# Batch attention of a four-layer tower: who forms the elementwise products, and where the weighted sums stand on TensorE

## The chip, the cores and the metric

The program runs on one core of a Trainium2 chip, in one launch. Its engines are TensorE (PE: matmuls, with weight loads as PEld), VectorE (DVE), ScalarE (ACT), GpSimd (POOL) and SyncE (SP). They run side by side and wait for each other by semaphores. The metric is device time in microseconds. The kernel before was timed three times: 2326.43, 2315.5 and 2321.1 us, median 2321.1 us.

## The reference, cut to what matters

The model is a tower of eight layers on activations `h` of 8 sequences x 512 tokens x 128. The change touches the seventh alone, an attention of 8 heads of 16. Its first axis is called the sequence, but it receives the 8 sequences as that axis, so each of the 512 token positions attends among 8 vectors only:

```python
def _L3_attn_ref(emb, W, b):
    L, B, E = emb.shape                      # 8, 512, 128
    scaling = (E / N_HEAD) ** (-0.5)
    ft = jnp.einsum('lbe,oe->lbo', emb, W) + b
    ft = ft.reshape(L, B * N_HEAD, 3 * HEAD_DIM).transpose(1, 0, 2)
    q, k, v = jnp.split(ft, 3, axis=-1)
    scores = jnp.einsum('bld,bmd->blm', q, k) * scaling
    mask = scores == 0
    attn = jax.nn.softmax(jnp.where(mask, -jnp.inf, scores), axis=-1)
    attn = jnp.where(mask, jnp.zeros((), attn.dtype), attn)
    out = jnp.einsum('blm,bmd->bld', attn, v)
    return out.transpose(1, 0, 2).reshape(L, B, E)
...
h = h + _L3_attn_ref(_layernorm(h, axis=-1), L3_attn_W, L3_attn_b)
```

## The kernel before, in words

`batch_attention` works in four chunks `c` of 128 token positions. An 8 x 8 attention per position and head is too small for a matmul, so it is done with elementwise products and sums:

- **Key products** (L2174): for each query `l` of 8, one DVE multiplication of the keys of all 8 positions `m` with query `l`, 128 x 1024 numbers, into `KM`. The first four of chunk 0 are made at the end of the layer before.
- **Scores** (L2293): TensorE sums each product over the 16 numbers of a head, by a matmul with a window of ones (`head_win`). One group of eight matmuls for `l` 0 to 3 (half 0), one for `l` 4 to 7 (half 1), both into the bank `SP`.
- ScalarE copies the scores out (L2240), TensorE turns them by four transposes (L2303), and VectorE runs the softmax (L2193 to L2203), with the exponential on ScalarE (L2244).
- **Weighted values** (L2209): for each `l`, one DVE multiplication of the values with the weights, 128 x 1024, into `big`.
- **Sums** (L2313): eight matmuls with the identity for each half, one for each `m` (called `k` in the code), add the products over `m` in a bank of PSUM. VectorE adds the bank to `h` (L2162).
- For chunk c+1 the layer norm is computed on VectorE beside this (L147 to L161, then `vector_scale`, L168), with a power on GpSimd (L184). TensorE then turns the normed tiles and projects to queries, keys and values (L2262 to L2279), and ScalarE copies them out (L2221 to L2235).

Nothing here is scheduled by a planner: each engine's queue is the order in which the code is written, and an instruction that waits holds up all behind it. On VectorE chunk c's queue is: key products of c, statistics of c+1, the two additions of c-1, `vector_scale` of c+1, softmax of c, weighted values of c. On TensorE it is: scores of c, transposes, projection of c+1, all 16 sums of c. GpSimd has nothing but the power. In the text, T0 is the moment at which a chunk's first weighted value starts on VectorE, right after L2203.

Of the kernel before, what the change touches and what calls it, by code (L numbers as in the profile page):

```python
# [16 lines left out]
ALU = mybir.AluOpType  # L17
# [3 lines left out]
P = 128  # L21
B, T, D = 8, 512, 128
NC_ = T // P
NT = B * NC_
NH = 8
DH = D // NH
# [2073 lines left out]
def batch_attention(ctx, nc, m):  # L2100
# [22 lines left out]
    norm = Norm(ctx, nc, m, "ba")  # L2123
    xt_ps, xt_sb, q_ps, q_sb, k_ps, k_sb, v_ps, v_sb = (sig(n, 2) for n in ("xt_ps", "xt_sb", "q_ps", "q_sb", "k_ps", "k_sb", "v_ps", "v_sb"))
    qk, sc_ps, sh_sb, sct_ps, st, ex_in, ex_sb = sig("qk", L), sig("sc_ps", 2), sig("sh_sb", 1), sig("sct_ps", 1), sig("st", 8), sig("ex_in", 1), sig("ex_sb", 1)
    pv, sum_ps, h_sb = sig("pv", L), sig("sum_ps", 2), sig("h_sb", 2)
    norm_m = Norm(ctx, nc, m, "cp")
    MX = [m.big[:, s * T:(s + 1) * T].rearrange("p (c d) -> p c d", c=NC_) for s in S]
# [4 lines left out]
    lmh = lambda v: v.rearrange("p (l m h) -> p l m h", l=L, m=L)  # L2133

    XC = [m.t512c[1][:, s, :] for s in S]
    made = lambda c, k: qk.at(c, k) - L // 2

    def chunk(c):

# [3 lines left out]
    with nc.Block() as block:  # L2143
# [4 lines left out]

        @block.gpsimd
        def _(pool):  # L2150
            for c in range(1, NC_):
                norm.gpsimd(pool, c - 1)
            norm_m.gpsimd(pool, 0)

        @block.vector
        def _(dve):

            def add(c):
                for half in S:
                    dve.wait_ge(sum_ps.sem, sum_ps.at(c, half + 1))  # L2160
                    h = H4[:, 4 * half:4 * half + 4, c, :]
                    nc.vector.tensor_tensor(h, h, OUT[half][:, :].rearrange("p (l d) -> p l d", d=D), ALU.add).then_inc(h_sb.sem, 1)  # L2162
                    if c == NC_ - 1 and half == 0:
                        dve.wait_ge(h_sb.sem, h_sb.at(c, 1))
                        norm_m.vector(dve, 0, norm_m.pair(0), MX)

            for c in range(NC_):
                for l in range(0 if c else L // 2, L):
                    if c and l % 4 == 0:
                        dve.wait_ge(q_sb.sem, q_sb.at(c - 1, l // 4 + 1))  # L2170
                    if c and l == 0:
                        dve.wait_ge(k_sb.sem, k_sb.at(c - 1, 2))
                        dve.wait_ge(sc_ps.sem, sc_ps.at(c - 1, 2))
                    nc.vector.tensor_tensor(QK[l].rearrange("p (m t) -> p m t", m=L), KT.rearrange("p (m t) -> p m t", m=L),  # L2174
                                            QT[:, l * P:(l + 1) * P].rearrange("p (o t) -> p o t", o=1).broadcast_to([P, L, P]),
                                            ALU.mult).then_inc(qk.sem, 1)
                if c + 1 < NC_:
                    norm.vector_stats(dve, c, chunk(c + 1))
                    norm.vector_aggr(dve, c)
                if c:  # L2180
                    add(c - 1)
                if c + 1 < NC_:
                    norm.vector_scale(dve, c, chunk(c + 1), XN)

                n = [0]

                def link(ins):
                    n[0] += 1
                    ins.then_inc(st.sem, 1)
                    dve.wait_ge(st.sem, st.at(c, n[0]))  # L2190

                dve.wait_ge(sct_ps.sem, sct_ps.at(c, 1))
                link(nc.vector.tensor_scalar(MK, SPT[:, :], 0.0, None, ALU.is_equal))  # L2193
                link(nc.vector.scalar_tensor_tensor(SC, MK, -3e38, SPT[:, :], ALU.mult, ALU.add))
                link(nc.vector.tensor_reduce(by_lh(mx[:, :]), by_m(SC), AX.X, ALU.max))
                nc.vector.tensor_tensor(lmh(SC), lmh(SC), wide_m(mx[:, :]), ALU.subtract).then_inc(ex_in.sem, 1)
                link(nc.vector.tensor_scalar(some[:, :], mx[:, :], -1e38, None, ALU.is_gt))
                dve.wait_ge(ex_in.sem, ex_in.at(c, 1))
                dve.wait_ge(ex_sb.sem, ex_sb.at(c, 1))
                link(nc.vector.tensor_reduce(by_lh(mx[:, :]), by_m(EX), AX.X, ALU.add))  # L2200
                link(nc.vector.reciprocal(mx[:, :], mx[:, :]))
                link(nc.vector.tensor_tensor(mx[:, :], mx[:, :], some[:, :], ALU.mult))
                link(nc.vector.tensor_tensor(lmh(EX), lmh(EX), wide_m(mx[:, :]), ALU.mult))  # L2203
                dve.wait_ge(v_sb.sem, v_sb.at(c, 2))
                for l in range(L):
                    pl = EX[:, slot(l) * L * NH:(slot(l) + 1) * L * NH].rearrange("p (n o) -> p n o", o=1).broadcast_to([P, L * NH, DH])
                    if c and l % 4 == 0:
                        dve.wait_ge(sum_ps.sem, sum_ps.at(c - 1, l // 4 + 1))
                    nc.vector.tensor_tensor(PR[l].rearrange("p (n x) -> p n x", x=DH), V[c % 2].rearrange("p (n x) -> p n x", x=DH),  # L2209
                                            pl, ALU.mult).then_inc(pv.sem, 1)  # L2210
            add(NC_ - 1)
            dve.wait_ge(h_sb.sem, h_sb.at(NC_ - 1, 2))

        @block.scalar
        def _(act):
# [22 lines left out]
            for c in range(NC_):  # L2238
                act.wait_ge(sc_ps.sem, sc_ps.at(c, 2))
                nc.scalar.copy(SH, SP[:, :]).then_inc(sh_sb.sem, 1)  # L2240
                if c + 1 < NC_:
                    turned(c + 1)
                act.wait_ge(ex_in.sem, ex_in.at(c, 1))
                nc.scalar.activation(EX, SC, ACT.Exp, scale=DH ** -0.5).then_inc(ex_sb.sem, 1)  # L2244
                if c + 1 < NC_:
                    project(c + 1)
            for s in S:
                act.wait_ge(mt_ps.sem, s + 1)
# [3 lines left out]
        def _(pe):  # L2252
# [3 lines left out]
            def project(c):  # L2256
# [12 lines left out]
                    nc.tensor.matmul(KP[s][:, :], w["b_w"][:, D:2 * D], XT[s][:, :], start=True, stop=True).then_inc(k_ps.sem, 1)  # L2269
                values(c)  # L2270

            def values(c):
                for s in S:
                    if c:
# [8 lines left out]

            for c in range(NC_):
                for half in S:
                    if c or half:
                        pe.wait_ge(qk.sem, made(c, 4 * half + 4))
                    if c and half == 0:
                        pe.wait_ge(sh_sb.sem, sh_sb.at(c - 1, 1))
                    for b in S:  # L2290
                        o = 24 - 16 * half - 8 * b
                        for g in range(4):
                            last = nc.tensor.matmul(SP[32 * g:32 * g + 32, :], w["head_win"][:, o:o + 32],  # L2293
                                                    QK[4 * half + g].rearrange("p (a b t) -> p a b t", b=2, t=P)[:, :, b, :],
                                                    start=half == 0 and b == 0, stop=half == 1 and b == 1)
                    last.then_inc(sc_ps.sem, 1)
                    if c == 0 and half == 0:
                        values(0)
                pe.wait_ge(sh_sb.sem, sh_sb.at(c, 1))
# [4 lines left out]
                last.then_inc(sct_ps.sem, 1)  # L2304
                if c + 1 < NC_:
                    project(c + 1)
                for half in S:
                    pe.wait_ge(pv.sem, pv.at(c, 4 * half + 4))
                    if c:
                        pe.wait_ge(h_sb.sem, h_sb.at(c - 1, half + 1))  # L2310
                    every = m.big[:, 4 * half * L * D:4 * (half + 1) * L * D].rearrange("p (l m d) -> p l m d", l=4, m=L)
                    for k in range(L):
                        last = nc.tensor.matmul(OUT[half][:, :].rearrange("p (l d) -> p l d", d=D), w["ident"][:, :], every[:, :, k, :],  # L2313
                                                start=k == 0, stop=k == L - 1)
                    last.then_inc(sum_ps.sem, 1)
            for s in S:
                pe.wait_ge(norm_m.ready.sem, s + 1)
                for k in range(NC_):
# [559 lines left out]
```

## Time and profile before

| | |
|---|---|
| median of 3 runs | 2321.1 us |
| the profiled execution, its span | 2301.55 us, 2300.5 us |
| busy PE, DVE, ACT, POOL | 81%, 76%, 57%, 14% |
| instructions | 31597 |
| mean granted TensorE clock | 0.9 of full |
| the batch attention, from the first key product to the last transposes | 1869.0 to 2007.7 us |

The batch attention is 6% of the span. The profile's page is an average over eight layers and says little of it, so the rows below are of its stretch, and of the few places elsewhere where GpSimd runs elementwise instructions beside VectorE. Each line of a timeline begins with the start and the length in us; one line may hold several instructions (x8), and its end in brackets is the idle time of the engine just before it and what released it. Where a matmul is of 32-bit floats each appears as two instructions, so 16 sums are x32.

### The profile page before, as it was taken

How to read it: one execution, taken by the hardware profiler on the slowest of the kernel's cores; microseconds unless marked ns; L12 is line 12 of the kernel's file. 1: busy time of each engine (PE TensorE's matmuls, PEld its weight loads, DVE VectorE, ACT ScalarE, POOL GpSimd, SP SyncE). 2: the span in 40 equal slices, each digit the busy share in tenths (PEclk: the TensorE clock that was granted, in tenths of full speed). 3: DMA queues.
4: the chain of work that ended last, by engine and by line, in shares of the span. 5: the costliest groups of instructions: out<-in, count | busy, mean ns of one | idle time of the engine just before them, and what ended most of it. 6: DMA issues, size and time to landing. Idle time of an engine off the chain costs nothing. (4 is left out here: it accounts for less than half of the span.)

```text
span 2300.5 us, 31597 instructions
## 1 busy us (share of the span) xinstructions
PE 1857.3 (81%) x11676; PEld 960.1 (42%) x11676; DVE 1748.0 (76%) x4911; ACT 1316.6 (57%) x1459; POOL 327.9 (14%) x392
## 2 busy tenths in 40 slices
PE   4999998888766688999989999899999979654930
PEld 1566654676421123344333344333344554332620
DVE  1677557577777789999999999999999778784532
ACT  0222222222236999999999999999999721010310
POOL 6000012010234000000000000000000000055256
PEclk8889999787688999999999999999999989867975
DMA  5400000000001100000000000000000000042632
GB/s 181 161 1 18 21 1 29 1 1 1 1 0 33 65 1 1 1 1 1 1 1 1 1 1 1 1 1 1 1 1 1 1 4 1 5 178 79 198 96 73
DMA packets 39658, 67.08 MB, mean 29 GB/s; under 512 B 7744, under 2 KB 27728, under 8 KB 38736
## 3 DMA queue, kind: packets, MB, share of 16 engines
q1 hardware_dynamic: 30768, 41.96, 5.4%
q0 software_dynamic: 8736, 23.10, 3.2%
q8 instruction: 93, 1.52, 0.3%
q14 instruction: 61, 0.50, 0.1%
HBM read 39.87 MB, written 23.07 MB: 27 GB/s over the span
## 5 line engine op out<-in xcount | busy, mean ns | idle before, releaser
L1929 ACT ACTIVATE KM<-KM 128x2048 f32<-128x2048 f32 x290 | 538.8, 1908 | 8.0 <-DMA w_a_ba<-in_a_ba 7.2
L1754 DVE TENSOR_SCALAR KM<-big 128x512 f32<-128x512 f32 x1160 | 480.3, 482 | 35.4 <-PE bank L2067 29.1
L2067 PE MATMUL bank<-KM,w_a_wa 128*32 128x512 f32 x2736 | 377.8, 626 | 90.7 <-ACT KM L1929 69.2
L184 POOL TENSOR_TENSOR nrstd<-nrstd,minus_half 128x4 f32<-128x4 f32 (+1 forms) x80 | 82.3, 1050 | 1759.9 <-DVE nrstd L161 1759.7
L1929 ACT ACTIVATE aa_args<-aa_args 128x2048 f32<-128x2048 f32 x142 | 266.0, 1909 | 1.5 <-DVE aa_args L1754 1.5
L1754 DVE TENSOR_SCALAR aa_args<-big 128x512 f32<-128x512 f32 x568 | 236.1, 482 | 12.9 <-PE bank L2067 12.3
L2067 PE MATMUL bank<-aa_args,w_a_wa 128*32 128x512 f32 x1360 | 185.7, 619 | 43.6 <-ACT aa_args L1929 31.3
L2067 PEld LDWEIGHTS bank<-KM,w_a_wa 128*32 128x32 f32 x2736 | 54.7, 109 | 240.9 <-ACT KM L1929 136.9
L2039 PE MATMUL bank<-XT,rf_wgu 128*128 128x256 f32 x512 | 145.0, 406 | 0.0
L2033 PE MATMUL bank<-XT,rf_wgu 128*128 128x256 f32 x512 | 142.7, 401 | 2.3 <-DVE ST L1825 2.3
L1926 ACT ACTIVATE KM<-big 128x512 f32<-128x512 f32 x208 | 132.8, 717 | 0.0
L2039 PEld LDWEIGHTS bank<-XT,rf_wgu 128*128 128x128 f32 x512 | 88.8, 193 | 97.8 <-issue 78.1
L2033 PEld LDWEIGHTS bank<-XT,rf_wgu 128*128 128x128 f32 x512 | 87.7, 189 | 94.9 <-issue 84.7
L1825 DVE SCALAR_TENSOR_TENSOR ST<-ST,bank 128x512 f32<-128x512 f32 x128 | 87.6, 684 | 46.2 <-ACT ST L1919 45.9
L1919 ACT ACTIVATE ST<-bank 128x512 f32<-128x512 f32 x128 | 75.8, 592 | 48.8 <-PE bank L2039 48.8
L2027 PEld LDWEIGHTS bank<-rf_wd,ST 128*128 128x128 f32 x512 | 62.3, 191 | 49.8 <-issue 48.3
L2313 PE MATMUL bank<-big,w_ident 128*128 128x512 f32 x128 | 63.3, 657 | 20.8 <-DVE big L2209 20.8
L2027 PEld LDWEIGHTS bank<-rf_wd,t512b 128*128 128x128 f32 x512 | 63.3, 193 | 37.3 <-issue 36.9
L1838 DVE SCALAR_TENSOR_TENSOR h<-bank,rf_w,h 128x128 f32<-128x128 f32 x256 | 77.4, 345 | 0.7 <-PE bank L2027 0.7
L583 ACT COPY KM<-bank 128x512 f32<-128x512 f32 x32 | 17.2, 593 | 104.2 <-PE bank L743 104.2
L2067 PEld LDWEIGHTS bank<-aa_args,w_a_wa 128*32 128x32 f32 x1360 | 27.0, 108 | 117.9 <-ACT aa_args L1929 69.6
L2027 PE MATMUL bank<-rf_wd,ST 128*128 128x128 f32 x512 | 73.6, 287 | 0.8 <-DVE ST L1831 0.8
(405 smaller groups left out, 3116.2 us busy)
## 6 DMA issues: line engine op xcount, KB each, us to landing
queues<-zeros SPq DMA_DIRECT2D x1, 8192.0 KB, 25.3
KM<-queues SPq DMA_DIRECT2D x32, 256.0 KB, 3.0
results<-KM POOLq DMA_DIRECT2D x32, 256.0 KB, 3.4
w<-in_w SPq DMA_DIRECT2D x1, 4096.0 KB
big<-in_w_pairs SPq DMA_DIRECT2D x1, 4096.0 KB
mf_tv<-in_task_W SPq DMA_DIRECT2D x1, 2048.0 KB, 8.4
la_v<-in_task_W SPq DMA_DIRECT2D x1, 2048.0 KB, 8.7
big<-XN SPq DMA_DIRECT2D x8, 256.0 KB, 2.6
```

The costliest lines, as they stand in the source:

```text
L184: self.nc.gpsimd.tensor_tensor(self.m.nrstd[s][:, 0:self.tiles], self.m.nrstd[s][:, 0:self.tiles], self.m.minus_half[:, 0:self.tiles], ALU ...
L1754: last = nc.vector.tensor_scalar(ARG(n, step)[:, cc, :], KU[:, i * T:(i + 1) * T], q, None, ALU.add)
L1825: nc.vector.scalar_tensor_tensor(TH(e), TH(e), 1.0, GATE(e)[:, :], ALU.add, ALU.mult).then_inc(a1_sb.sem, 1)
L1838: last = nc.vector.scalar_tensor_tensor(h, OUT(e)[:, s * D:(s + 1) * D], WT[:, s, e:e + 1], h, ALU.mult, ALU.add)
L1919: nc.scalar.activation(TH(e), GATE(e)[:, :], ACT.Tanh, scale=0.5).then_inc(th_sb.sem, 1)
L1926: last = nc.scalar.activation(ARG(n, step)[:, cc, :], KU[:, i * T:(i + 1) * T], ACT.Tanh, bias=query(n, step, cc))
L1929: last = nc.scalar.activation(ARG(n, step), ARG(n, step), ACT.Tanh)
L2027: last = nc.tensor.matmul(OUT(e)[:, s * D:(s + 1) * D], AC(e)[:, o:o + P], wd[:, e, a, :], start=a == 0, stop=a == HB - 1)
L2033: last = nc.tensor.matmul(LIFT(e)[:, a * TOK:(a + 1) * TOK], wgu[:, e, 1, a, :], XMT[parity][:, 0:TOK], start=True, stop=True)
L2039: last = nc.tensor.matmul(GATE(e)[:, a * TOK:(a + 1) * TOK], wgu[:, e, 0, a, :], XMT[parity][:, 0:TOK], start=True, stop=True)
L2067: last = nc.tensor.matmul(m.bank[g][32 * cc:32 * cc + 32, :], w["a_wa"][:, 30 - 2 * k:62 - 2 * k], ARG(n, step)[:, cc, :], start=k == 0, s ...
L2313: last = nc.tensor.matmul(OUT[half][:, :].rearrange("p (l d) -> p l d", d=D), w["ident"][:, :], every[:, :, k, :], start=k == 0, stop=k == ...
```

## The change

Two of the eight key products (`l` = 3 and 7, list `PL`) and two of the eight weighted values of each chunk go from VectorE to GpSimd. The first group of chunk 0 stays on VectorE. GpSimd's products signal by semaphores of their own (`qk_pool`, `pv_pool`), for which TensorE and ScalarE now wait too. The 16 sums of a chunk, which stood in one piece, are divided: all of half 0 and the first two of half 1 stay in their place, three go behind the first group of the next chunk's scores and three behind the second. After the last chunk all 16 still stand together.

```diff
+    qk_pool, pv_pool = sig("qk_pool", 2), sig("pv_pool", 2)
+    DL, PL = [l for l in range(L) if l % 4 != 3], [3, 7]
-    made = lambda c, k: qk.at(c, k) - L // 2
+    made = lambda c, half: L // 2 + len(DL) * (c - 1) + len(DL) // 2 * (half + 1)
         def _(pool):
-            for c in range(1, NC_):
-                norm.gpsimd(pool, c - 1)
+            for c in range(NC_):
+                if c:
+                    for half, l in enumerate(PL):
+                        pool.wait_ge(q_sb.sem, q_sb.at(c - 1, half + 1))
+                        if half == 0:
+                            pool.wait_ge(k_sb.sem, k_sb.at(c - 1, 2))
+                            pool.wait_ge(sc_ps.sem, sc_ps.at(c - 1, 2))
+                        nc.gpsimd.tensor_tensor(QK[l]..., KT..., QT..., ALU.mult).then_inc(qk_pool.sem, 1)
+                if c + 1 < NC_:
+                    norm.gpsimd(pool, c)
+                for half, l in enumerate(PL):
+                    if half == 0:
+                        pool.wait_ge(st.sem, st.at(c, 8))
+                        pool.wait_ge(v_sb.sem, v_sb.at(c, 2))
+                    if c:
+                        pool.wait_ge(sum_ps.sem, sum_ps.at(c - 1, half + 1))
+                    nc.gpsimd.tensor_tensor(PR[l]..., V[c % 2]..., pl, ALU.mult).then_inc(pv_pool.sem, 1)
...
-                for l in range(0 if c else L // 2, L):
+                for l in (DL if c else range(L // 2, L)):
...
-                for l in range(L):
+                for l in DL:
...
+                if c:
+                    act.wait_ge(pv_pool.sem, pv_pool.at(c - 1, 2))
                 nc.scalar.activation(EX, SC, ACT.Exp, scale=DH ** -0.5).then_inc(ex_sb.sem, 1)
                 if c + 1 < NC_:
+                    if c:
+                        act.wait_ge(qk_pool.sem, qk_pool.at(c - 1, 2))
                     project(c + 1)
...
+            def sums(c, half, ks):
+                every = m.big[:, 4 * half * L * D:4 * (half + 1) * L * D]...
+                for k in ks:
+                    if k == 0:
+                        pe.wait_ge(pv.sem, len(DL) * c + len(DL) // 2 * (half + 1))
+                        pe.wait_ge(pv_pool.sem, pv_pool.at(c, half + 1))
+                        if c:
+                            pe.wait_ge(h_sb.sem, h_sb.at(c - 1, half + 1))
+                    last = nc.tensor.matmul(OUT[half]..., w["ident"][:, :], every[:, :, k, :], start=k == 0, stop=k == L - 1)
+                if k == L - 1:
+                    last.then_inc(sum_ps.sem, 1)
...
                 for half in S:
-                    if c or half:
-                        pe.wait_ge(qk.sem, made(c, 4 * half + 4))
+                    if c:
+                        pe.wait_ge(qk.sem, made(c, half))
+                        pe.wait_ge(qk_pool.sem, qk_pool.at(c - 1, half + 1))
...
                     last.then_inc(sc_ps.sem, 1)
+                    if c:
+                        sums(c - 1, 1, ((2, 3, 4), (5, 6, 7))[half])
...
-                for half in S:
-                    pe.wait_ge(pv.sem, pv.at(c, 4 * half + 4))
...
+                sums(c, 0, range(L))
+                sums(c, 1, (0, 1) if c + 1 < NC_ else range(L))
```

On TensorE, from the end of a projection to the next, the queue before reads as follows (L2279 is the projection's last matmul, L2313 the sums, L2293 the scores, L2303 the transposes of the scores, L2262 those of the next projection):

```order
L2279 MATMUL bank<-w_b_b,w_first_row 128x512
L2313 MATMUL bank<-big,w_ident 128x512 x16
L2293 MATMUL bank<-KM,w_head_win 32x512 x16
L2303 MATMUL bank<-w_ident,t512b 128x8x16 x4
L2262 MATMUL bank<-w_ident,XN 128x128 x8
```

The same place in the changed program's queue on TensorE (the sums are now L2305 and the scores L2334):

```order
L2317 MATMUL bank<-w_b_b,w_first_row 128x512
L2305 MATMUL bank<-big,w_ident 128x512 x10
L2334 MATMUL bank<-KM,w_head_win 32x512 x8
L2305 MATMUL bank<-big,w_ident 128x512 x3
L2334 MATMUL bank<-KM,w_head_win 32x512 x8
L2305 MATMUL bank<-big,w_ident 128x512 x3
L2346 MATMUL bank<-w_ident,t512b 128x8x16 x4
L2287 MATMUL bank<-w_ident,XN 128x128 x8
```

Six of the sixteen sums now stand behind scores, and the last three of them ahead of the transposes.

On GpSimd, in the whole of the layer, only powers stood (first row below); in the changed program the products stand between them (L2172 weighted values, L2160 key products):

```order
-L184 TENSOR_TENSOR nrstd<-nrstd,minus_half 128x4 x8
+L184 TENSOR_TENSOR nrstd<-nrstd,minus_half 128x4 x2
+L2172 TENSOR_TENSOR big<-big,t512b 128x1024 x2
+L2160 TENSOR_TENSOR KM<-big 128x1024 x2
+L184 TENSOR_TENSOR nrstd<-nrstd,minus_half 128x4 x2
+L2172 TENSOR_TENSOR big<-big,t512b 128x1024 x2
+L2160 TENSOR_TENSOR KM<-big 128x1024 x2
```

Four products stand in a row behind a softmax: two weighted values of chunk c and two key products of chunk c+1.

On VectorE the same two steps follow each other behind the softmax's last instruction, before (L2209, L2174):

```order
L2203 TENSOR_TENSOR t512b<-t512b,ba_mx 128x512
L2209 TENSOR_TENSOR big<-big,t512b 128x1024 x8
L2174 TENSOR_TENSOR KM<-big 128x1024 x8
L147 BN_STATS nstat<-h 128x6 x8
```

and in the changed program (L2230, L2195):

```order
L2224 TENSOR_TENSOR t512b<-t512b,ba_mx 128x512
L2230 TENSOR_TENSOR big<-big,t512b 128x1024 x6
L2195 TENSOR_TENSOR KM<-big 128x1024 x6
L147 BN_STATS nstat<-h 128x6 x8
```

Sixteen products became twelve, with nothing else moved on this engine.

## Rows read from the trace of the kernel before

**Rows 1.** Timeline of TensorE in the batch attention: sums and scores.

```profile
1894.38 16.85 PE L2313 MATMUL bank<-big,w_ident 128*128 128x512 f32 x32 [3.12 <-DVE big L2209]
1911.16 3.64 PE L2293 MATMUL bank<-KM,w_head_win 128*32 128x512 f32 x32
...
1927.62 15.60 PE L2313 MATMUL bank<-big,w_ident 128*128 128x512 f32 x32 [3.10 <-DVE big L2209]
...
1959.60 14.00 PE L2313 MATMUL bank<-big,w_ident 128*128 128x512 f32 x32 [3.11 <-DVE big L2209]
1973.54 3.64 PE L2293 MATMUL bank<-KM,w_head_win 128*32 128x512 f32 x32
...
1989.96 16.84 PE L2313 MATMUL bank<-big,w_ident 128*128 128x512 f32 x32 [11.42 <-DVE big L2209]
```

**Rows 2.** Timeline of VectorE: weighted values, key products, additions, scale, first of the softmax.

```profile
1889.69 9.17 DVE L2209 TENSOR_TENSOR big<-big,t512b 128x1024 f32<-128x1024 f32 x8
...
1911.27 0.69 DVE L2162 TENSOR_TENSOR h<-h,bank 128x512 f32<-128x512 f32 x1 [0.37 <-PE bank L2313]
1911.87 2.14 DVE L168 TENSOR_SCALAR XN<-h,nmv,nrstd 128x128 f32<-128x128 f32 x8
1916.20 0.69 DVE L2193 TENSOR_SCALAR t512a<-bank 128x512 f32<-128x512 f32 x1 [2.19 <-PE bank L2303]
...
1922.93 9.17 DVE L2209 TENSOR_TENSOR big<-big,t512b 128x1024 f32<-128x1024 f32 x8
1932.02 9.17 DVE L2174 TENSOR_TENSOR KM<-big 128x1024 f32<-128x1024 f32 x8
...
1948.18 0.69 DVE L2193 TENSOR_SCALAR t512a<-bank 128x512 f32<-128x512 f32 x1 [1.39 <-PE bank L2303]
...
1954.92 9.17 DVE L2209 TENSOR_TENSOR big<-big,t512b 128x1024 f32<-128x1024 f32 x8
...
1978.57 0.69 DVE L2193 TENSOR_SCALAR t512a<-bank 128x512 f32<-128x512 f32 x1 [4.20 <-PE bank L2303]
...
1985.28 9.17 DVE L2209 TENSOR_TENSOR big<-big,t512b 128x1024 f32<-128x1024 f32 x8
```

**Rows 3.** Groups by shape on GpSimd over the whole span: busy us, mean ns.

```profile
L1032 POOL TENSOR_TENSOR KM<-KM 128x256 f32<-128x256 f32 x32 | 23.2, 726 | 15.2 <-ACT KM L1287 15.2
L1034 POOL TENSOR_TENSOR KM<-KM 128x128 f32<-128x128 f32 x32 | 14.7, 459 | 2.5
L305 POOL TENSOR_TENSOR h<-h,mf_ln 128x512 f32<-128x512 f32 x8 | 10.7, 1344 | 8.7 <-DVE mf_x L438 8.4 <-DVE XN L438 0.3
```

**Rows 4.** Timelines of VectorE and GpSimd near 620 us.

```profile
617.86 0.28 DVE L1095 TENSOR_TENSOR be_gates<-be_gates,be_colsum 128x128 f32<-128x128 f32 x1
622.38 0.85 DVE L1095 TENSOR_TENSOR be_gates<-be_gates,be_colsum 128x128 f32<-128x128 f32 x1
...
622.35 0.73 POOL L1032 TENSOR_TENSOR KM<-KM 128x256 f32<-128x256 f32 x1
623.16 0.46 POOL L1034 TENSOR_TENSOR KM<-KM 128x128 f32<-128x128 f32 x1
```

**Rows 5.** Timelines of VectorE and GpSimd near 371 us.

```profile
371.21 2.66 DVE L444 TENSOR_SCALAR mf_gb<-w_ones,mf_gate_first,w_gate_row 128x128 f32<-128x128 f32 x2
...
371.12 2.67 POOL L305 TENSOR_TENSOR h<-h,mf_ln 128x512 f32<-128x512 f32 x2
```

**Rows 6.** The instructions of L1095, L444 and L1153: shortest, median, longest (ns).

```profile
L1095 DVE TENSOR_TENSOR be_gates<-be_gates,be_colsum x16: 273/293/849, 542.4 to 652.8; 128x128 f32<-128x128 f32 x16
...
L444 DVE TENSOR_SCALAR mf_gb<-w_ones,mf_gate_first,w_gate_row x8: 333/1291/1382, 295.5 to 372.5; 128x128 f32<-128x128 f32 x8
...
L1153 DVE SCALAR_TENSOR_TENSOR h<-bank,be_weights,h x128: 252/342/352, 615.5 to 711.8; 128x128 f32<-128x128 f32 x128
```

**Rows 7.** Busy time in stretches: us, PE, PEld, DVE, ACT, POOL, granted clock, DMA.

```profile
1977.20:1990.00 12.80, 0.69 (x5) 0.46 (x5) 10.50 (x14) 1.22 (x2) 0.00 (x0) 0.69 0.01 1
1990.00:1998.00 8.00, 8.00 (x12) 3.43 (x13) 4.45 (x4) 0.00 (x0) 0.00 (x0) 0.64 0.00 0
```

More of the change, by code:

```diff
@@ L2150, in _ @@
         def _(pool):
[L2151 to L2152 removed]
+            for c in range(NC_):
[5 more added lines that the diff above has]
+                            pool.wait_ge(sc_ps.sem, sc_ps.at(c - 1, 2))
+                        nc.gpsimd.tensor_tensor(QK[l].rearrange("p (m t) -> p m t", m=L), KT.rearrange("p (m t) -> p m t", m=L),
+                                                QT[:, l * P:(l + 1) * P].rearrange("p (o t) -> p o t", o=1).broadcast_to([P, L, P]),
+                                                ALU.mult).then_inc(qk_pool.sem, 1)
+                if c + 1 < NC_:
[6 more added lines that the diff above has]
+                        pool.wait_ge(sum_ps.sem, sum_ps.at(c - 1, half + 1))
+                    pl = EX[:, slot(l) * L * NH:(slot(l) + 1) * L * NH].rearrange("p (n o) -> p n o", o=1).broadcast_to([P, L * NH, DH])
+                    nc.gpsimd.tensor_tensor(PR[l].rearrange("p (n x) -> p n x", x=DH), V[c % 2].rearrange("p (n x) -> p n x", x=DH),
+                                            pl, ALU.mult).then_inc(pv_pool.sem, 1)
             norm_m.gpsimd(pool, 0)
@@ L2270, in project @@
                 values(c)
+            def sums(c, half, ks):
+                every = m.big[:, 4 * half * L * D:4 * (half + 1) * L * D].rearrange("p (l m d) -> p l m d", l=4, m=L)
+                for k in ks:
[4 more added lines that the diff above has]
+                            pe.wait_ge(h_sb.sem, h_sb.at(c - 1, half + 1))
+                    last = nc.tensor.matmul(OUT[half][:, :].rearrange("p (l d) -> p l d", d=D), w["ident"][:, :], every[:, :, k, :],
+                                            start=k == 0, stop=k == L - 1)
+                if k == L - 1:
+                    last.then_inc(sum_ps.sem, 1)
             def values(c):
@@ L2285, in _ @@
                 for half in S:
-                    if c or half:
-                        pe.wait_ge(qk.sem, made(c, 4 * half + 4))
+                    if c:
+                        pe.wait_ge(qk.sem, made(c, half))
+                        pe.wait_ge(qk_pool.sem, qk_pool.at(c - 1, half + 1))
+                    elif half:
+                        pe.wait_ge(qk.sem, L // 2)
                     if c and half == 0:
@@ L2306, in _ @@
                     project(c + 1)
-                for half in S:
-                    pe.wait_ge(pv.sem, pv.at(c, 4 * half + 4))
[L2309 to L2315, printed above, removed]
+                sums(c, 0, range(L))
+                sums(c, 1, (0, 1) if c + 1 < NC_ else range(L))
             for s in S:
```

## The prediction

> **What bounds the kernel now.** The page's shares cover eight layers, so I read the timelines of the batch attention's own stretch. First TensorE [rows 1]: of the 16 sums of a chunk the shortest piece takes 14.00 us, and the scores begin as soon as they are through (1911.16 and 1973.54). Then VectorE [rows 2]: the weighted values begin at T0 = 1889.69, 1922.93, 1954.92 and 1985.28, and the sums about 4.69 us later, when four products are there (1894.38 - 1889.69). Behind the scores VectorE waits 2.19, 1.39 and 4.20 us before the next softmax. So the loop of a chunk is: four products on VectorE, 16 sums, 32 rows of scores, transposes, softmax; TensorE is its longest piece and VectorE has one to four us of slack. From T0 to the next softmax are 26.51, 25.25 and 23.65 us (1916.20 - 1889.69 and so on); the differences are the sums, 16.85, 15.60 and 14.00 us. Behind the last T0 comes only 4.68 us to the sums, and the sums.
>
> **The change, part by part.**
>
> *Taken from VectorE.* Eight products take 1932.02 - 1922.93 = 9.09 us [rows 2], so one is a step of 1.14 us. Two fewer of each kind save 4.55 us of busy VectorE in a full chunk. The path has only the first three of each half in it: by this alone sums could start at 3 x 1.14 = 3.4 us behind T0 instead of 4.69.
>
> *Added on GpSimd.* No row has a GpSimd product of 1024 numbers. 128, 256 and 512 numbers take 459, 726 and 1344 ns [rows 3]. The first step's slope (267 ns per 128) gives 1344 + 4 x 267 = 2.41 us as the lower bound, twice the largest 2.69 as the upper one; continuing the last slope, 309 ns per 128, gives 2.58 us. I take 2.5 us, between them and nearest to the largest row. The Trainium skill (GPSIMD Engine Reference, Elementwise side-by-side) has 4497 ns for 2048 numbers; by half of that, 2.25 us, the sum below would be some 3 us smaller.
>
> *What it costs VectorE.* A product has both inputs in SBUF. So has L1095, and its rows are the ones to look at [rows 4]: alone it takes 0.28 us, but started 0.03 us behind a GpSimd product of 0.73 us it takes 0.85, and ends 0.15 us behind that product. It did not run slower, it stood until the product was 0.12 to 0.13 us from its end (622.38 + 0.85 - 0.28 = 622.95, against 623.08). L444 shows the same against the larger GpSimd product: two of them last exactly as long as two of L305 [rows 5], 1291 ns in the median against 333 undisturbed, while L1153 (only one input tensor in SBUF) is never above 352, with GpSimd's products beside it in the same stretch [rows 6]. So I charge each GpSimd product to VectorE as a block of 2.5 - 0.13 = 2.4 us. Bounds: nothing, if products this long don't block (rival 2), and 2.69 us. The Trainium skill (SBUF, Who interferes with whom) says that a VectorE instruction with two SBUF inputs and a GpSimd one that reads SBUF exclude each other, and that the second fully blocks. Rows 4 to 6 agree where GpSimd came first; none shows VectorE first with an instruction of 1.2 us. By the rule GpSimd then waits for one product and takes the next turn, as in the forecast.
>
> *Turns.* In [rows 5] each L444 got in between two GpSimd products (two lasted 2.66, not one 0.3 and one 2.6), so I let the engines take turns. Behind a softmax GpSimd has four products in a row, VectorE twelve. With VectorE first its third product ends at 3 x 1.14 + 2 x 2.4 = 8.2 us behind T0, its sixth at 6 x 1.14 + 4 x 2.4 = 16.4, its third key product at 19.8 and its sixth at 23.3. GpSimd has finished its four by then. Before, the eighth key product ended at 18.2: so four moved products save 4.55 us and cost 9.6.
>
> *TensorE with that,* at 14.00/16 = 0.875 us a sum and 1.82 us a half of the scores [rows 1]: eight sums from 8.3 to 15.3; two of half 1 wait for 16.4 and end at 18.2; scores half 0 wait for 19.8 and end at 21.7; three sums to 24.3; scores half 1 to 26.1; three sums to 28.8.
>
> *Sums behind the scores.* VectorE's addition needs the last sum, and `vector_scale`, behind it in the queue, comes ahead of the softmax. Before, that was covered by scores and transposes. Measured from the last sum (1911.16) to the end of the scale (1911.87 + 2.14 = 1914.01) it is 2.85 us, now in the open. It takes the place of the 1.4 us in which the scores were copied and turned (1911.16 + 3.64 to 1916.20); these now lie beside the three last sums and the scale. So the next softmax starts at 28.8 + 2.85 = 31.6 us. Where the sums run as slowly as in the first two gaps (16.85 and 15.60 for 16), the six late ones add 1.1 and 0.6: 32.7 and 32.2. Before the last softmax there is no scale, only 0.8 us for the addition: 29.6.
>
> *Sum.* 32.7 - 26.5 = 6.2; 32.2 - 25.25 = 6.9; 29.6 - 23.65 = 6.0; behind the last T0 the sums start at 8.3 instead of 4.7, 3.6 us, and half 1 is then covered (its products are there at 6 x 1.14 + 2 x 2.4 = 11.6). Together 22.7 us. The new waits of ScalarE cost nothing: they are for products a whole chunk old. GpSimd's power comes behind key products that are done 10 us earlier. No DMA moves. The profiled execution's 2301.55 us (span 2300.5 and 1.05 around it) becomes 2324.3. The median of the runs shown is 19.5 us above that execution, from no part of this stretch that I can name, so I add the sum to it: 2321.1 + 22.7 = 2344.
>
> On the path lie 3 x 4 + 2 = 14 blocks, so the bounds of a block (2.3 to 2.6 us) are 2 us less and 3 us more. TensorE's clock may add: while it idled for most of 12.8 us its granted clock was 0.69, and 0.64 in the next 8 us [rows 7]. Its idle time ahead of the sums grows here from 3.1 to nearly 7 us. At 0.64 the eight sums of half 0 take 10.9 instead of 7.0 us, end at 19.2, and push what follows by 1 us a chunk, 3 us in all. The forecast's own range is 2336 to 2354.
>
> **Rivals.**
> 1. *GpSimd gets no turn.* VectorE's products start every 1.14 us though each lasts 1.22 (eight in 9.17, less seven steps) [rows 2]: if the next one always holds the way already, GpSimd starts only when twelve are through, at 13.7. Half 0's sums start at 16.2 and end at 23.2, two more 24.9, scores 26.7, sums 29.4, scores 31.2, sums 33.8, softmax 36.7. The gaps grow by 11.3 (with the slow sums), 12.0 and 11.0, the tail by 4.7 (6.8 + 2.5 against 4.7): 39 us, 2360. Against it: GpSimd's product in [rows 5] lasted its usual 1.3 us among VectorE's.
> 2. *The products run side by side* (not slower). One mechanism: a long GpSimd product leaves VectorE its reads. Then sums start at 3.5 us, and TensorE runs through: 3.5 + 20.5 + 2.85 = 26.85 (+0.3), 3.5 + 19.2 + 2.85 = 25.6 (+0.3), 3.5 + 17.6 + 0.85 = 22.0 (-1.7), tail -1.2: -2.3 us, 2319. Even the full relief of VectorE brings so little because TensorE sets the loop and the late sums expose the scale. It decides from blocks below about 0.3 us. For it: no row has products of this length; against it all of [rows 4 to 6].
> 3. *The change does not relieve what it says:* the products block, but GpSimd is first after the softmax, and three of its products come before VectorE's third. The sums then start at 10.6, but half 1 still waits for 16.4, and 10.6 + 7.0 = 17.6 is only 1.2 behind that; scores half 0 wait for 19.8 in both. Only the tail grows, 0 to 1 us: 2345, within the forecast's range.
>
> **How the numbers follow.** Turns, with rival 3: 0.73, at 2344. No turn for GpSimd: 0.09, at 2360. Side by side: 0.13, at 2319. The rest, 0.05, is a block much smaller than the product, for example 1 us: 14 x 1.4 less, 2325. No change by measurement is within 0.5%, 11.6 us, so 2309.5 to 2332.7. Slower by more: the turns and the first rival, 0.82. Within: 0.16. Faster: 0.02, since nothing above gains more than 2.3 us. The range leaves out side by side and a little above: 2325 to 2363.
>
> **What would show it.** Right: VectorE's weighted values and key products that meet a GpSimd product last about 3.5 us instead of 1.22, four in each full chunk and two in the last; GpSimd's about 2.5, or up to 3.7 where they wait themselves; the sums start 8 us behind T0; TensorE waits ahead of the second half's sums and the first half's scores; ahead of the softmax VectorE waits for sums (L2183's line), not for transposes. Wrong: VectorE's products all at 1.22 with GpSimd busy beside them (then 2319), GpSimd's four beginning only behind VectorE's twelve (2360), or GpSimd products far from 2.5 us, which moves the sum by 14 us for each us.

## The result and the profile after

The changed kernel takes 2333.62 us (median of 14 runs, 2324.71 to 2345.16), the kernel before 2321.74 us in the same comparison (14 runs). The ratio is 1.0059, with a 95% interval of 1.0041 to 1.0076: 0.6% slower, some 10 to 18 us. Forecast were 2344 us, 22.7 us slower, range 2325 to 2363. The direction, the mechanism and the wide range hold; the size was forecast 1.7 times too large (22.7 against 13.7 us by the ratio), and the time lies below the range of 2336 to 2354 that the forecast gave for its own mechanism alone.

The profiled executions differ by more (span 2329.7 against 2300.5 us), but half of that lies outside the changed layer. I therefore read the layer itself, with two measures: a *gap*, from T0 to the next softmax, and the *three loops*, from the first T0 to the fourth.

Timeline of VectorE in the changed kernel, answering to [rows 2] (start, length, engine, line; L2230 weighted values, L2195 key products, L2183 additions, L2214 the softmax's first):

```profile
1891.78 14.79 DVE L2230 TENSOR_TENSOR big<-big,t512b 128x1024 f32<-128x1024 f32 x6
1906.49 6.89 DVE L2195 TENSOR_TENSOR KM<-big 128x1024 f32<-128x1024 f32 x6
1913.31 1.63 DVE L147 BATCH_NORM_STATS2 nstat<-h 128x6 f32<-128x128 f32 x8
...
1919.39 0.69 DVE L2183 TENSOR_TENSOR h<-h,bank 128x512 f32<-128x512 f32 x1 [3.06 <-PE bank L2305]
1920.00 2.14 DVE L168 TENSOR_SCALAR XN<-h,nmv,nrstd 128x128 f32<-128x128 f32 x8
1922.05 0.69 DVE L2214 TENSOR_SCALAR t512a<-bank 128x512 f32<-128x512 f32 x1
...
1928.77 14.79 DVE L2230 TENSOR_TENSOR big<-big,t512b 128x1024 f32<-128x1024 f32 x6
...
1959.04 0.68 DVE L2214 TENSOR_SCALAR t512a<-bank 128x512 f32<-128x512 f32 x1
...
1965.77 14.79 DVE L2230 TENSOR_TENSOR big<-big,t512b 128x1024 f32<-128x1024 f32 x6
...
1993.99 0.68 DVE L2214 TENSOR_SCALAR t512a<-bank 128x512 f32<-128x512 f32 x1
...
2000.69 10.37 DVE L2230 TENSOR_TENSOR big<-big,t512b 128x1024 f32<-128x1024 f32 x6
```

Six weighted values take 14.79 us where eight took 9.17. The six key products behind them take 6.89, their own speed: by then GpSimd is through. The softmax has no wait of its own any more; the wait (3.06 us) stands ahead of the second addition, with the scale behind it. The gaps are 30.27, 30.27 and 28.22 us against 26.51, 25.25 and 23.65; the three loops 108.91 against 95.59 us, 13.3 more.

GpSimd's timeline in the same stretch (two instructions to a row):

```profile
1891.83 5.84 POOL L2172 TENSOR_TENSOR big<-big,t512b 128x1024 f32<-128x1024 f32 x2 [11.97 <-DVE t512b L2224]
1897.63 6.72 POOL L2160 TENSOR_TENSOR KM<-big 128x1024 f32<-128x1024 f32 x2
```

And the products of both engines over the whole layer, each line's shortest, median and longest in ns:

```profile
L2230 DVE TENSOR_TENSOR big<-big,t512b x24: 1209/2946/3433, 1891.8 to 2009.8; 128x1024 f32<-128x1024 f32 x24
L2160 POOL TENSOR_TENSOR KM<-big x6: 3369/3398/3418, 1897.6 to 1974.9; 128x1024 f32<-128x1024 f32 x6
L2172 POOL TENSOR_TENSOR big<-big,t512b x8: 2905/2937/2970, 1891.8 to 2003.7; 128x1024 f32<-128x1024 f32 x8
```

On both engines a product lasts 2.9 us beside weighted values and 3.4 beside keys: each row contains its own work and the wait for the other's turn. The first five of VectorE's products of chunk 0 and the first and third of GpSimd's, one line each:

```profile
L2230 DVE TENSOR_TENSOR big<-big,t512b x1: 1225/1225/1225, 1891.8 to 1891.8; 128x1024 f32<-128x1024 f32 x1
L2230 DVE TENSOR_TENSOR big<-big,t512b x1: 2953/2953/2953, 1892.9 to 1892.9; 128x1024 f32<-128x1024 f32 x1
L2230 DVE TENSOR_TENSOR big<-big,t512b x1: 2947/2947/2947, 1895.8 to 1895.8; 128x1024 f32<-128x1024 f32 x1
L2230 DVE TENSOR_TENSOR big<-big,t512b x1: 3409/3409/3409, 1898.7 to 1898.7; 128x1024 f32<-128x1024 f32 x1
L2230 DVE TENSOR_TENSOR big<-big,t512b x1: 3433/3433/3433, 1902.0 to 1902.0; 128x1024 f32<-128x1024 f32 x1
L2172 POOL TENSOR_TENSOR big<-big,t512b x1: 2969/2969/2969, 1891.8 to 1891.8; 128x1024 f32<-128x1024 f32 x1
L2160 POOL TENSOR_TENSOR KM<-big x1: 3369/3369/3369, 1897.6 to 1897.6; 128x1024 f32<-128x1024 f32 x1
```

VectorE's first product runs at its own speed (1.2 us) although GpSimd's first begins 0.05 us behind it; the next two last 2.95, the next two 3.4, the sixth 1.2. That is the picture of turns: under sharing the first would have been slowed too.

TensorE, answering to [rows 1] (L2305 sums, L2334 scores, L2346 transposes):

```profile
1898.80 10.59 PE L2305 MATMUL bank<-big,w_ident 128*128 128x512 f32 x20 [5.46 <-DVE big L2230]
1910.04 1.92 PE L2334 MATMUL bank<-KM,w_head_win 128*32 128x512 f32 x16 [0.64 <-DVE KM L2195]
1911.89 2.84 PE L2305 MATMUL bank<-big,w_ident 128*128 128x512 f32 x6
1914.66 1.92 PE L2334 MATMUL bank<-KM,w_head_win 128*32 128x512 f32 x16
1916.52 2.84 PE L2305 MATMUL bank<-big,w_ident 128*128 128x512 f32 x6
1919.19 0.60 PE L2346 MATMUL bank<-w_ident,t512b 128*128 128x128 f32 x4
...
2007.70 15.90 PE L2305 MATMUL bank<-big,w_ident 128*128 128x512 f32 x32 [13.92 <-DVE big L2230]
```

The sums start 7.02 us behind T0 instead of 4.69, the scores wait again for VectorE's key products (0.64 us), and the transposes come last. The ten sums have no wait among them: the eight of half 0 ran so slowly that half 1's products (ready at 1891.78 + 14.79 = 1906.57) were there when they ended. So one forecast sign, TensorE waiting ahead of the second half's sums, did not appear. Behind the last T0 the sums start 2.33 us later and run 0.94 us shorter (15.90 against 16.84).

### The profile page after: what moved, and what is told of

The parts are those of the page before. It is cut to its first block and busy times, and to the rows that moved or that the text cites. A ratio compares the mean times of both kernels' runs of the same rounds, so it can differ in the third digit from the quotient of the medians.

```text
span 2329.7 us, 31614 instructions
## 1 busy us (share of the span) xinstructions
PE 1862.0 (80%) x11676; PEld 958.6 (41%) x11676; DVE 1759.1 (76%) x4897; ACT 1316.5 (57%) x1459; POOL 370.5 (16%) x406
## 5 line engine op out<-in xcount | busy, mean ns | idle before, releaser
L2305 PE MATMUL bank<-big,w_ident 128*128 128x512 f32 x128 | 65.2, 665 | 29.1 <-DVE big L2230 29.1
```

## The experiments

The theory: two products with both inputs in SBUF exclude each other on VectorE and GpSimd, and the engines take turns; on top of that the late sums put the scale in the open. Rivals: the order of the sums does all the harm; the engines slow each other by sharing; any product blocks any other. Eight kernels were run, in two groups of four. "First sums" is behind T0 (in the row of serial, gaps and first sums count from GpSimd's first product). Ratios are to the kernel before in the same group; the groups ran on two chips (before: 2322.81 and 2285.4 us), so between groups only ratios and traces are compared. Gaps and loops are each of one execution, and in how many gaps the sums run slowly differs (16.85, 15.60 and 14.00 us before). A difference of 2 or 3 us in the loops can come from that alone.

| kernel | gaps, us | three loops | first sums | ratio (95%) |
|---|---|---|---|---|
| before | 26.51, 25.25, 23.65 | 95.59 | 4.69 | 1 |
| changed | 30.27, 30.27, 28.22 | 108.91 | 7.02 | 1.0059 (1.0041 to 1.0076) |
| serial | 35.44, 34.87, 32.47 | 123.07 | 12.10 | 1.0115 (1.0071 to 1.0159) |
| one_input | 26.04, 24.34, 23.98 | 94.52 | 3.54 | 0.9968 (0.9945 to 0.9991) |
| sums_only | 28.37, 25.78, 23.74 | 98.04 | 4.69 | 1.0005 (0.9980 to 1.0031) |
| pool_only | 27.41, 27.41, 27.40 | 102.40 | 7.02 | 1.0017 (0.9987 to 1.0047) |
| scale_mid | 28.15, 28.79, 28.10 | 105.20 | 7.01 | 1.0057 (1.0036 to 1.0079) |
| late_sums | 24.44, 23.64, 24.40 | 92.59 | 4.69 | 0.9992 (0.9977 to 1.0007) |
| no_block | 24.33, 24.34, 22.28 | 91.31 | 3.53 | 0.9976 (0.9955 to 0.9997) |
| no_block_late | 20.40, 20.40, 20.40 | 81.54 | 3.54 | 0.9940 (0.9920 to 0.9961) |

### The products one after the other (serial)

```diff
                 dve.wait_ge(v_sb.sem, v_sb.at(c, 2))
+                dve.wait_ge(pv_pool.sem, pv_pool.at(c, 2))
+                if c + 1 < NC_:
+                    dve.wait_ge(qk_pool.sem, qk_pool.at(c, 2))
                 for l in DL:
```

> As the changed kernel, but VectorE waits ahead of its weighted values until GpSimd's four products (two behind the last softmax) are through, so that each runs alone. Theory (the two exclude each other, a GpSimd product holds VectorE for 1.8 us with weights and 2.3 us with keys, and the rest of its 2.9 and 3.4 us is its own waiting): alone they last 1.9 to 2.0 and 2.3 to 2.5 us, VectorE's all 1.22, and the twelfth VectorE product ends about 22.5 us behind the softmax, under 1 us later than in the changed kernel (21.6); the whole is 5 to 9 us slower than the changed kernel, because the first sums start at 12 instead of 7 us. Rival (they slow each other by sharing, 2.9 and 3.4 us are GpSimd's own lengths): alone still 2.9 and 3.4, twelfth product at 26.5.

Shortest, median and longest in ns, GpSimd's products and VectorE's weighted values, when none meets another:

```profile
L2172 POOL TENSOR_TENSOR big<-big,t512b x8: 1931/1932/1936, 1900.5 to 2025.4; 128x1024 f32<-128x1024 f32 x8
L2160 POOL TENSOR_TENSOR KM<-big x6: 2340/2340/2341, 1904.2 to 1990.4; 128x1024 f32<-128x1024 f32 x6
L2233 DVE TENSOR_TENSOR big<-big,t512b x24: 1218/1219/1227, 1909.0 to 2033.6; 128x1024 f32<-128x1024 f32 x24
```

This is the number that the prediction lacked: a GpSimd product of 1024 numbers is 1.93 us with weights and 2.34 us with keys, not 2.5. The rival of sharing falls: 2.9 and 3.4 us are not GpSimd's own lengths. From the first GpSimd product to the end of the twelfth of VectorE's are 22.26 us here (1900.46 to 1915.83 + 6.89) and 21.60 in the changed kernel (1891.78 to 1906.49 + 6.89). Running both at once saves 0.66 us in 22: next to nothing is parallel.

The whole was slower than I expected: the three loops are 14.2 us longer than the changed kernel's, not 5 to 9 (the ratios differ by 0.0056, 13 us, with intervals too wide to tell it from 9). The miss is TensorE: its first ten sums took 11.39, 10.72 and 10.38 us where I had counted 8.75, the first at a granted clock of 0.77 after 10.6 us without work (below).

### One input in SBUF (one_input)

VectorE's first input is taken from the bank `SPT` of PSUM, read twice over, for all weighted values and for the key products of chunks 1 to 3:

```diff
-  tensor_tensor(PR[l]..., V[c % 2]..., pl, ALU.mult)
+  tensor_tensor(PR[l]..., SPT..., pl, ALU.mult)
-  tensor_tensor(QK[l]..., KT..., QT[l]..., ALU.mult)
+  tensor_tensor(QK[l]..., SPT..., QT[l]..., ALU.mult)
```

> As the changed kernel, but VectorE's products of chunks 1 to 3's keys and all weighted values read their first input from a bank of PSUM (the turned scores, twice over) instead of SBUF, so they have one input in SBUF; the numbers they make are not the reference's. Theory (the shared thing is the second SBUF input): VectorE's products last about 1.2 us with GpSimd's beside them, GpSimd's are as long as alone (1.9 to 2.5), the sums start 3.5 us behind the first weighted value, gaps 25.6 to 26, 25.6 and 22 us, the whole within 3 us of the kernel before. Rival (any two products on the two engines block each other, or VectorE's writes do): VectorE's products at 2.9 to 3.4 us and the changed kernel's gaps of 28 to 30 us.

The same measure, VectorE's two lines and GpSimd's two:

```profile
L2237 DVE TENSOR_TENSOR big<-bank,t512b x24: 1214/1215/1225, 1892.0 to 1992.2; 128x1024 f32<-128x1024 f32 x24
L2200 DVE TENSOR_TENSOR KM<-bank,big x18: 1215/1215/1215, 1898.8 to 1968.3; 128x1024 f32<-128x1024 f32 x18
...
L2172 POOL TENSOR_TENSOR big<-big,t512b x8: 1932/1932/1935, 1892.0 to 1988.4; 128x1024 f32<-128x1024 f32 x8
L2160 POOL TENSOR_TENSOR KM<-big x6: 2354/2397/2436, 1895.8 to 1962.0; 128x1024 f32<-128x1024 f32 x6
```

Same place, same sizes, same writes to SBUF, and not one VectorE product is blocked; GpSimd's are as long as alone, or 0.1 us more. That puts the cause down to the second input from SBUF. What the Trainium skill says (SBUF, Who interferes with whom), that one such input does not contend and that two contend with a GpSimd instruction that reads SBUF, is shown here at products of 1.2 and 1.9 to 2.4 us. (No run has a GpSimd product that does not read SBUF.) In sum the time agrees with the forecast's rival 2 (products side by side): three loops 1.1 us shorter than before and first sums 1.15 us earlier, where rival 2 had 1.1 and 1.2. The agreement of the loops is luck: gap by gap it is -0.5, -0.9 and +0.3 us where rival 2 had +0.3, +0.3 and -1.7. Rival 2 had the late sums slow in the first two gaps; here they are all fast, and the first ten are slow (10.55 instead of 8.85 us) in the first and third. The whole is 7 us faster than before by the ratio, with an interval of 2 to 13, expected within 3.

### The order of the sums alone (sums_only), GpSimd's products alone (pool_only)

```diff
 # sums_only
-    DL, PL = [l for l in range(L) if l % 4 != 3], [3, 7]
+    DL, PL = list(range(L)), []      # and the waits for qk_pool and pv_pool taken out
 # pool_only
-                    if c:
-                        sums(c - 1, 1, ((2, 3, 4), (5, 6, 7))[half])
-                sums(c, 1, (0, 1) if c + 1 < NC_ else range(L))
+                sums(c, 1, range(L))
```

> All eight products of each kind stay on VectorE; only the order of the sums is that of the changed kernel. Theory (the blocks of GpSimd's products cost, and the late sums by themselves give nothing, because they expose the scale): from a chunk's first weighted value to the next softmax about 25.6, 25.6 and 23.5 us (before 26.5, 25.25, 23.65; changed kernel 30.3, 30.3, 28.2), the sums start 4.7 us behind the first weighted value, and the whole is within 2 us of the kernel before. Rival (the order of the sums is what costs most): gaps of 28 us and more in the first two, a loss of 5 us or more against before. Rival (the late sums do bring time): gaps below 24.5 us.

> GpSimd makes its two products of each kind, but all 16 sums of a chunk stand together again ahead of the next scores. Theory (blocks alone): the sums start 7.0 us behind the first weighted value; half 1's products are there at 14.8, so 16 sums end at 21.9, scores at 25.5, softmax at 26.9 us with fast sums, up to 28.5 with slow ones; each gap 1.5 to 3.3 us longer than before, tail 2.3 longer, in all 8 to 10 us slower than before and some 6 us faster than the changed kernel. Rival (the two parts just add, and the order of the sums costs nothing): 14 to 16 us slower than before, like the changed kernel.

The order of the sums alone costs 2.45 us in three loops, nothing that the times can tell. Where all sums run at full speed the gap is 25.78 us (the second) against 23.65 before (the third), 2.1 us more; the slow sums of the kernel before hide part of it. Its place is as expected: VectorE's timeline in sums_only has the scale directly ahead of the softmax,

```profile
1956.23 0.69 DVE L2183 TENSOR_TENSOR h<-h,bank 128x512 f32<-128x512 f32 x1 [1.93 <-PE bank L2300]
1956.84 2.14 DVE L168 TENSOR_SCALAR XN<-h,nmv,nrstd 128x128 f32<-128x128 f32 x8
1958.89 0.69 DVE L2214 TENSOR_SCALAR t512a<-bank 128x512 f32<-128x512 f32 x1
```

and what the earlier scores win is spent on it. Its first gap was 2.8 us longer than expected, because ten sums took 11.73 us there and 8.85 in the others.

GpSimd's products alone cost 6.81 us in the loops and 2.3 at the last first sums; expected were 8 to 10 in all, the ratio says 4 us with an interval of -3 to +11. Both edits together cost 13.3, more than 2.45 + 6.81. Of the missing 4 us two causes can be read. The first, VectorE's and TensorE's rows of pool_only:

```profile
1941.13 6.89 DVE L2195 TENSOR_TENSOR KM<-big 128x1024 f32<-128x1024 f32 x6
...
1951.48 2.14 DVE L168 TENSOR_SCALAR XN<-h,nmv,nrstd 128x128 f32<-128x128 f32 x8
1953.81 0.69 DVE L2214 TENSOR_SCALAR t512a<-bank 128x512 f32<-128x512 f32 x1 [0.19 <-PE bank L2344]
...
1948.77 3.64 PE L2334 MATMUL bank<-KM,w_head_win 128*32 128x512 f32 x32
```

There VectorE's queue, delayed by the blocks, still fits beside TensorE's scores and transposes, to 0.19 us, and the scores, behind all 16 sums, wait for no key product. The blocks reach TensorE only as 2.33 us ahead of the first sums. With the late sums the scores stand behind ten sums and do wait for VectorE's key products, which the blocks delay by twice as much, from 13.7 to 18.2 us behind T0. The wait is already there in sums_only,

```profile
1946.87 1.92 PE L2328 MATMUL bank<-KM,w_head_win 128*32 128x512 f32 x16 [0.23 <-DVE KM L2195]
```

so the whole delay goes through: between sums_only and the changed kernel the second and third gaps differ by 4.5 us each (25.78 and 30.27, 23.74 and 28.22). The second cause is the clock: the slow sums of the kernel before make the first two gaps of pool_only look cheap (27.41 against 26.51 and 25.25, but 27.40 against 23.65 in the third). How the 4 us divide was not measured.

### The scale between the additions (scale_mid)

```diff
                 if c:
-                    add(c - 1)
+                    add(c - 1, [0])
                 if c + 1 < NC_:
                     norm.vector_scale(dve, c, chunk(c + 1), XN)
+                if c:
+                    add(c - 1, [1])
```

> The changed kernel, with the scale of the next chunk's norm moved between the two additions on VectorE. Theory (the scale stands in the open behind the last sum, 2.1 us in each of the first two gaps): softmax begins 0.8 instead of 2.7 us behind the last sum, gaps 28.2, 28.2 and 28.2 us instead of 30.3, 30.3 and 28.2, the whole 4 us faster than the changed kernel. Rival (the softmax waits for something else, the blocks of GpSimd's products): gaps unchanged.

The loops became 3.71 us shorter (4.2 expected; in the second gap slow sums, 11.88 us for ten, took 0.6 back), so the exposed scale is worth that much in the changed kernel. The times can't confirm it: 1.0057 with an interval of 1.0036 to 1.0079 is no different from the changed kernel's. It is shown by the trace alone.

### Spread sums with nothing waiting for the last (late_sums)

No products on GpSimd, and against the changed kernel:

```diff
-                        sums(c - 1, 1, ((2, 3, 4), (5, 6, 7))[half])
+                        sums(c - 1, 1, ((2, 3, 4), (5,))[half])
                 last.then_inc(sct_ps.sem, 1)           # the transposes
+                if c:
+                    sums(c - 1, 1, (6, 7))
 # VectorE: addition of half 0, scale; the addition of half 1 inside the softmax,
                 link(nc.vector.tensor_scalar(some[:, :], mx[:, :], -1e38, None, ALU.is_gt))
+                if c:
+                    add(c - 1, [1])
                 dve.wait_ge(ex_in.sem, ex_in.at(c, 1))
```

> No product on GpSimd. Three sums of half 1 between the two groups of scores, one behind them, two behind the transposes; scale ahead of the second addition, and that addition inside the softmax where VectorE waits for the exponential. Theory (the idea of spreading the sums is sound once nothing waits for the last of them): softmax starts behind scores and transposes at 22.2 us or behind VectorE's scale at 23.4 us, gaps 23.4, 23.4 and 22.2 us against 26.5, 25.25 and 23.65 before, 6 us faster than before, 2 us less where the sums run slowly. Rival (TensorE is the bound, whatever stands where): gaps within 1 us of before.

Half of what was expected: loops 3.0 us shorter, the ratio 0.9992 is not told from 1. The second gap, with fast sums, is near its 23.4 (23.64), but the kernel before has 23.65 where its sums are fast (its third gap). In the others the sums were slow again, and there the gap is 24.4 us, against 26.51 before: by these gaps, what this order gives is mainly that slow first sums no longer lie on the path in full. Busy time in the three stretches of the ten sums (length; PE, PEld, DVE, ACT, POOL; the first number behind POOL's is the granted clock):

```profile
1884.30:1895.90 11.60, 11.60 (x20) 4.81 (x20) 11.60 (x11) 0.00 (x0) 0.00 (x0) 0.75 0.01 1
1915.50:1924.20 8.70, 8.70 (x20) 3.67 (x20) 8.70 (x8) 0.00 (x0) 0.00 (x0) 1.00 0.00 0
1945.80:1957.40 11.60, 11.60 (x20) 4.78 (x20) 11.60 (x11) 0.00 (x0) 0.00 (x0) 0.75 0.00 0
```

TensorE had been idle for 3.12, 1.41 and 3.08 us ahead of them.

### Products that do not block, and the version that beats both (no_block, no_block_late)

This computes the reference's function, with one SBUF input for each of VectorE's products that can meet a GpSimd one: the softmax writes the weights of VectorE's six slots to PSUM and GpSimd's two to SBUF, and the query comes, with its bias, from the projection's own bank, for which the values move to banks 0 and 1, with the waits to match.

```diff
-    QP, KP, VP = [m.bank[2], m.bank[3]], [m.bank[0], m.bank[1]], [m.bank[2], m.bank[3]]
+    QP, KP, VP = [m.bank[2], m.bank[3]], [m.bank[0], m.bank[1]], [m.bank[0], m.bank[1]]
 # key products of chunks 1 to 3 on VectorE
+    scalar_tensor_tensor(QK[l]..., QP[l // 4][...l...], w["b_col"][:, 0:1], KT..., ALU.add, ALU.mult)
-    link(tensor_tensor(lmh(EX), lmh(EX), wide_m(mx), ALU.mult))
+    tensor_tensor(lmh(EX)[:, 6:8], lmh(EX)[:, 6:8], wide_m(mx)[:, 6:8], ALU.mult)   # GpSimd's weights
+    link(tensor_tensor(lmh(SPT)[:, 0:6], lmh(EX)[:, 0:6], wide_m(mx)[:, 0:6], ALU.mult))
-    pl = EX[...slot(l)...]
+    pl = SPT[...slot(l)...]
```

no_block_late adds the edits of late_sums.

> The changed kernel with the same results, but VectorE's products have only one input in SBUF: the weights of its six products are written to the scores' bank of PSUM, and the queries are read with their bias from the projection's bank. Theory (the second SBUF input is what is shared, not the products as such): VectorE's products at 1.2 us beside GpSimd's of 1.9 and 2.35 us, sums start 3.5 us behind the first weighted value, gaps about 26, 24.5 and 23.5 us, softmax 0.2 us longer, the whole 10 us faster than the changed kernel and 1 to 3 us faster than before, within what can be told. Rival (the form reading the queries from PSUM blocks too): key products at 3.4 us, gaps of 27 us and more.

> The products of the kernel above and the order of the sums and additions of late_sums together. Theory (each relieves the bound that stays in the other: VectorE's products there, the late sums here): softmax starts behind scores and transposes, at 20.6 us behind the first weighted value with fast sums, 22 with slow ones; three gaps of 20.6 to 22 us instead of 26.5, 25.25 and 23.65, tail 1.2 us shorter: 10 to 14 us faster than before, 0.4 to 0.6 per cent. Rival (TensorE's own work sets the loop): less than 7 us, no more than late_sums.

no_block is 0.24% faster than before, and its VectorE products run at their own speed beside GpSimd's. Its loops are 17.6 us shorter than the changed kernel's, where I had expected 10 for the whole, and 4.3 shorter than before: all its first ten sums ran at full speed (8.85 us), behind only 0.9 us without work. no_block_late takes 0.6% off the kernel before (0.9940, 0.9920 to 0.9961; 2271.06 against 2285.4 us in that group) and, by the two ratios, beats the changed kernel by 1.2%. Its loops are 14.05 us shorter than before, the upper end of what was expected (gaps of 20.4, expected 20.6 to 22), and together the two edits give more than 4.3 + 3.0. VectorE's timeline:

```profile
1909.30 6.87 DVE L2238 TENSOR_TENSOR big<-big,bank 128x1024 f32<-128x1024 f32 x6
1916.10 7.23 DVE L2196 SCALAR_TENSOR_TENSOR KM<-bank,w_b_col,big 128x1024 f32<-128x1024 f32 x6
...
1929.70 0.69 DVE L2219 TENSOR_SCALAR t512a<-bank 128x512 f32<-128x512 f32 x1 [0.90 <-PE bank L2352]
```

and TensorE's, from the sums on (L2340 scores, L2352 transposes):

```profile
1912.84 8.85 PE L2311 MATMUL bank<-big,w_ident 128*128 128x512 f32 x20
1921.62 1.92 PE L2340 MATMUL bank<-KM,w_head_win 128*32 128x512 f32 x16
1923.47 2.84 PE L2311 MATMUL bank<-big,w_ident 128*128 128x512 f32 x6
1926.25 1.92 PE L2340 MATMUL bank<-KM,w_head_win 128*32 128x512 f32 x16
1928.10 1.13 PE L2311 MATMUL bank<-big,w_ident 128*128 128x512 f32 x2
1929.06 0.60 PE L2352 MATMUL bank<-w_ident,t512b 128*128 128x128 f32 x4
```

There is no idle time in brackets: from the first sum to the transposes TensorE never waits, and all its sums of the three loops run fast (8.85/20 = 0.44 us a row; only the last sixteen, behind 8.61 us of idle time, are slow again, 15.92 us). In the first two loops TensorE has next to no room left: it is busy for 26.81 of the 27.20 us from 1909.30 to 1936.50. In the third, where there is no next chunk to project, it is busy for only 21.93 of 27.15 us, and the loop is no shorter. So what sets it is the chain of VectorE's first three products (3.54 us), TensorE's sums, scores and transposes (16.9 us to the next softmax), and the softmax itself (6.8 us).

## Why the prediction came out as it did

- **TensorE sets the loop, VectorE has little slack.** Right, as far as it was tried: with the products unblocked (one_input) the three loops together moved by 1 us only.
- **A GpSimd product blocks VectorE for its length less 0.13 us.** The mechanism is right. VectorE's twelve products ended at 21.60 instead of 13.7 us, 1.98 us for each block; GpSimd alone takes 2.14 in the mean of the four, less 0.13 is 2.0. The rows it was read from mix two cases: L1095 has two inputs from SBUF, but L444 [rows 5] is a TENSOR_SCALAR with one, and it too stood for 1.28 to 1.38 us instead of 0.33 beside L305. So two inputs are not the only thing that blocks; what lets L444 block was not tried.
- **A block is 2.4 us.** This is the term that was mis-sized. I stretched lengths of 128, 256 and 512 numbers to 1024 and put 2.41 us as the lower bound of the product; it is 1.93 and 2.34, both below it. The mistake was to start from the row of 512 numbers, an instruction of another kind whose 1344 ns are more than half of either product. From the row of 256 the same slope gives 726 + 6 x 267 = 2.33 us, the key product's length; the weights' is below any line through those rows. With 2.0 for 2.4 the prediction's own chain gives 21.7 for the twelfth product, 30.0 for the softmax with fast sums and 28.0 without the scale; measured were 21.6, 30.27 and 28.22. That is 1.6 us a chunk and 0.8 at the last, 5.6 of the 7.0 us by which the forecast's sum (22.7) is above the layer's own growth (13.3 + 2.3 = 15.7, before the last sums' 0.9 us back); most of the rest is the slowness forecast for the late sums, 1.7 us (below). The longer loops against the times: 14.7 us in the layer, 14 us by the ratio.
- **Turns.** Right, down to the order: VectorE first, then alternately. Rival 1 (no turn) and rival 3 (GpSimd first) did not occur.
- **The late sums expose the scale by 2.85 - 1.4 us.** Right in place and size: from the start of the transposes to the softmax 2.86 us (1922.05 - 1919.19), and scale_mid takes 3.7 us back.
- **The late sums run slowly where the early ones did,** 1.1 and 0.6 us. Wrong: every group of three sums took 2.84 us, full speed. Only the sums behind an idle stretch were slow, ten of them in 10.55 to 11.14 us instead of 8.85, and in this kernel those were covered, because the scores behind them had to wait for VectorE's third key product (18.2 us behind T0) in any case. My reserve of 3 us for a lower clock was not needed.
- **The whole with the median.** The layer (14.7 us) accounts for all of the measured difference; the 29 us between the two profiled spans would have misled. The measured time is inside the stated range because that range reached down to 2325, for a block much smaller than the product; by the forecast's own mechanism it was to be 2336 or more.

## What to carry to other kernels

Before work goes from VectorE to GpSimd, count the inputs in SBUF: with two on VectorE beside such products on GpSimd the hoped-for parallelism is next to none, and a product moved from 1.14 to 2 us of exclusive time is a loss; with one of VectorE's inputs in PSUM the parallelism is real. A single input is shown to be free for the two multiplications tried here; L444 shows that it isn't for every instruction, so look at the form's own rows. When a piece of work is put behind something on one engine, look for what waits for its end on another: here an addition with a scale queued behind it. Two edits that each cost or give little can lock or unlock each other, so the second bound is to be lifted with the first.

## What the hardware showed that I had not expected

- GpSimd's multiplication of 1024 numbers a partition took 1.93 us where one input repeats each number 16 times, and 2.34 where the second input is a row of 128 read over again. Why was not tried.
- Exclusion is nearly complete even though a GpSimd product spends 1.6 to 2 times as long on a number as VectorE: 22.26 us in turn, 21.60 "at once".
- The first ten sums of a chunk took 8.85 us behind 0.9 or 1.41 us of idle TensorE, 8.85 or 10.55 behind 1.97 (both in one_input), 8.85 or 11.7 behind 3.1 (both in sums_only), 10.55 to 11.9 behind 4.3 to 5.5, and 10.4 to 11.4 behind 10.6. Granted clocks were 1.00 in the fast ones and 0.74 to 0.85 in the slow ones, so each slow group had a part at the lower of the clock's two levels, 1.2 instead of 2.4 GHz. The same kernel shows both behind equal idle time; what decides was not settled. It gives an unforeseen profit to filling the idle stretch: part of no_block_late's gain over late_sums is that its sums in the three loops are never slow.
